# ALiBi attention: both heads' products ahead of both mask records, on the diagonal blocks

## The reference, cut to what matters

```
scores = einsum('bqhd,bkhd->bhqk', q, k) * scale
bias   = slopes[:, None, None] * rel            # rel = key position - query position
scores = where(rel <= 0, scores + bias, -inf)   # causal
probs  = softmax(scores, axis=-1)
attn   = einsum('bhqk,bkhd->bqhd', probs, v)
```

## Time and profile before

| | us |
|---|---|
| median of three runs | 1590.12 (1585.02 to 1590.92) |
| the profiled execution | 1588.67 |
| its span | 1586.8 |
| its mean granted TensorE clock | 0.966 |
| PE busy | 1477.9 (93% of the span) |
| DVE busy | 893.4 (56%) |
| ACT busy | 805.4 (51%) |
| POOL busy | 549.5 (35%) |

### The profile page before, as it was taken

The page is one execution under the profiler, slowest core; times in us unless marked ns, Lnnn a source line. Parts: engine busy times, 40 slices in busy tenths (PEclk is TensorE's granted clock), DMA queues, the critical chain, the costliest instruction groups (busy, mean ns, idle before and its releaser), DMA issues. The chain is left out here.

```text
span 1586.8 us, 23991 instructions
## 1 busy us (share of the span) xinstructions
PE 1477.9 (93%) x8320; PEld 1036.9 (65%) x8320; DVE 893.4 (56%) x1346; ACT 805.4 (51%) x1731; POOL 549.5 (35%) x506
## 2 busy tenths in 40 slices
PE   5499999999999999999968988899999989999996
PEld 4377676667767766776635866555555548888885
DVE  3145454555544555554565745666666616877877
ACT  2266555556655555666423430455555565433343
POOL 0444433344443334444015044223232004444442
PEclk9699999999999999999978997999999999999998
DMA  3135544544454354445530034333333205000000
GB/s 120 49 46 51 50 34 47 42 40 43 48 50 34 46 47 40 39 46 41 84 60 1 1 44 69 48 55 55 55 55 55 88 2 226 1 1 0 1 27 27
DMA packets 46289, 74.06 MB, mean 47 GB/s; under 512 B 18704, under 2 KB 24848, under 8 KB 45328
## 3 DMA queue, kind: packets, MB, share of 16 engines
q1 hardware_dynamic: 41872, 62.70, 28.4%
q0 software_dynamic: 4352, 10.49, 4.4%
HBM read 40.39 MB, written 2.10 MB: 27 GB/s over the span
## 5 line engine op out<-in xcount | busy, mean ns | idle before, releaser
L677 DVE TENSOR_REDUCE nmax<-sc 128x1 f32<-128x128 f32 (+7 forms) x256 | 192.4, 752 | 182.7 <-PE sc L465 182.7
L1515 DVE TENSOR_REDUCE pm<-l_sm 128x2 f32<-128x1024 f32 (+1 forms) x192 | 179.8, 957 | 112.6 <-PE l_sm L1395 61.8
L1475 ACT ACTIVATE l_probs<-l_banks 128x512 f32<-128x512 f32 (+3 forms) x384 | 171.2, 493 | 136.1 <-PE l_banks L1419 97.1
L608 ACT COPY pt<-tb 128x512 f32<-128x512 f32 (+3 forms) x256 | 129.2, 505 | 201.4 <-PE tb L479 199.8
L600 ACT ACTIVATE probs<-sc,nmax 128x128 f32<-128x128 f32 (+7 forms) x256 | 190.6, 745 | 56.2 <-DVE nmax L677 55.9
L479 PE MATMUL tb<-ident,probs 128*128 128x128 f32 x1152 | 174.1, 276 | 2.1 <-ACT pt L608 1.1
L78 PE MATMUL sc<-k_h,q_h 128*128 128x512 f32 (+3 forms) x384 | 144.7, 377 | 22.1 <-POOL q_l L748 14.6
L1416 PE MATMUL l_banks<-qk_bufs 128*128 128x512 f32 (+3 forms) x384 | 141.3, 412 | 5.2 <-ACT l_probs L1475 3.8
L1392 PE MATMUL l_sm<-qk_bufs 128*128 128x512 f32 (+3 forms) x384 | 130.8, 412 | 12.9 <-DVE pm L1515 6.5
L503 PE MATMUL mb<-pt,ckv 128*64 128x512 f32 (+3 forms) x768 | 137.8, 494 | 0.1
L78 PE MATMUL sc<-k_l,q_h 128*128 128x512 f32 (+3 forms) x384 | 133.7, 348 | 0.0
(11 more groups left out here) (263 smaller groups left out, 3145.2 us busy)
## 6 DMA issues: line engine op xcount, KB each, us to landing
gated_late<-in_gated SPq DMA_DIRECT2D x11, 768.0 KB, 14.0
wout<-in_w_out SPq DMA_DIRECT2D x16, 512.0 KB, 7.1
late<-late SPq DMA_DIRECT2D x128, 64.0 KB, 2.0
rb<-rT SPq DMA_DIRECT2D x64, 128.0 KB, 8.8
qk_bufs<-late SPq DMA_DIRECT2D x96, 64.0 KB, 5.0
qk_bufs<-late POOLq DMA_DIRECT2D x96, 64.0 KB, 5.9
nope_t<-in_nope_by_dim SPq DMA_DIRECT2D x16, 192.0 KB, 5.6
late<-in_gated SPq DMA_DIRECT2D x3, 768.0 KB, 9.1
```

What stands on the lines that cost most here:

```text
L608: act.copy(pt[i // 4][:, e, j0:j0 + nb, (i % 4) * P:(i % 4 + 1) * P], tb[TB[g]][:, 0:nb, :]).then_inc(pt_act, 1)
L677: dve.tensor_reduce(nmax[:, n % 4:n % 4 + 1], sc[n % 2][:, 0:(n // 2 + 1) * P], AX.X, ALU.max, negate=True).then_inc(negmax, 1)
L1475: act.activation(probs[(NC * g + c) % RING][:, h, 0:w], banks[:, (E_STEPS * g + n) % SLOTS, 0:w], ACT.Exp).then_inc(exped, 1)
L1515: dve.tensor_reduce(pm[g % 2][:, :, s, i, half], slot(("m", g, n))[:, :, 0:w], AX.X, ALU.max, negate=True).then_inc(freed, 1)
```

## The change

In `m`, the two products of a diagonal unit come first and their two mask records behind them. In `e`, the products of two heads on a diagonal block are issued at the place of the even head (h0 or h2), then both mask records; the place of the odd head (h1 or h3) is empty. Work that the order puts between the two heads therefore follows behind the pair. Each mask record still raises `sE` once, so that ACT takes the same steps in the same order. Since the pair writes two banks, it waits at its first product until one more exponential is done: product n waits for exponential n-2, not n-3.

```diff
@@ -1391,7 +1391,8 @@
                     for par in range(2):
                         last = pe.matmul(dst[:, par, 0:w], queries(b, s)[:, i * P:(i + 1) * P], keys(b, 2 * s + par)[:, c0:c0 + w],
                                          start=True, stop=not diagonal)
-                        if diagonal:
+                    if diagonal:
+                        for par in range(2):
                             last = pe.matmul(dst[:, par, w - P:w], keep.ident_b[:], keep.mask[:], start=False, stop=True)
                     last.then_inc(scores, 1)
 
@@ -1411,12 +1412,19 @@
                         pe.wait_ge(rows_in, ROWS * (g + 1))
                         if g == 0:
                             pe.wait_ge(v_ev, ST)
-                    from_one(pe, exped, E_STEPS * g + n + 1 - SLOTS)
                     diagonal = q0 == j * P
-                    last = pe.matmul(banks[:, at, 0:w], keys(b, h)[:, j * P:(j + 1) * P], queries(b, h // 2)[:, q0:q0 + w],
-                                     start=True, stop=not diagonal)
+                    if diagonal and h % 2:
+                        return
+                    both = (h, h + 1) if diagonal else (h,)
+                    from_one(pe, exped, E_STEPS * g + n + len(both) - SLOTS)
+                    for x in both:
+                        last = pe.matmul(banks[:, (at + x - h) % SLOTS, 0:w], keys(b, x)[:, j * P:(j + 1) * P], queries(b, x // 2)[:, q0:q0 + w],
+                                         start=True, stop=not diagonal)
                     if diagonal:
-                        last = pe.matmul(banks[:, at, 0:P], keep.ident_b[:], keep.mask_t[:], start=False, stop=True)
+                        for x in both:
+                            last = pe.matmul(banks[:, (at + x - h) % SLOTS, 0:P], keep.ident_b[:], keep.mask_t[:], start=False, stop=True)
+                            if x == h:
+                                last.then_inc(sE, 1)
                     last.then_inc(sE, 1)
```

## The result

The changed kernel takes 1605.12 us (median; 1604.42 to 1606.65), the kernel before 1590.23 in the same comparison: 1.011 times, with a 95% interval of 1.0082 to 1.0137. The medians differ by 15 us, and the forecast was 1601. The profiled execution has a span of 1602.6 us, 15.8 more than before.

A forecast was written before the change was run, and what follows sets the result against it. PE was taken to bound the second pass, with short waits. Load cover -13.4, bank waits +23.1 and uncashed saving +2.0 make +11.7 us, forecast 1601; its own range 1595 to 1606, the 8-in-10 range 1594 to 1611.

The forecast's parts named there:

- What bounds the kernel: Attention stage: PE bounds the second pass, with short waits, and nothing behind the stage absorbs the difference.
- The load cover: Diagonal pairs in both passes: weight loads hidden behind neighbouring products save 0.02 to 0.07 us a pair, 13.4 us in all.
- The unknown price: A mask record behind a mask record on PE: taken as 0.06 us, the least possible, with 0.11 the next kind above.
- Units side by side: First-pass units that now follow each other wait for DVE's buffers: 2 us of the saving are not cashed.
- The wait for the banks: Second pass: a chunk's second pair waits for h0's exponential, 0.85 to 0.52 us by width; 23.1 us lost in all.
- The groups: Bank waits left after filling, per group: 2.87 us in groups 1, 3, 5; 2.86 in 0, 2, 4; 2.03 in 6.
- The last group: Group 7, with nothing to fill its bank waits: 3.90 us of them, the group some 3 us longer than 27.5.
- The first group: Group 0 of the second pass, counted like groups 2 and 4: 2.86 us lost to bank waits.
- no cover: Rival, chance 0.03: loads of a product behind a product are not hidden in the pair; +25 us, 1614.
- the dear mask record: Rival, chance 0.15: a mask behind a mask costs 0.11 us, each pair loses 0.05 more; 1610 us.
- no change: Rival, chance 0.15: bank waits run together with existing waits and half of the 23.1 us vanishes; 1589 us.
- faster: Rival, chance 0.05: bank waits cost nothing because the exponentials are done in time; 1577 us.

The follow-up runs named there:

- e1: Kernel before with only the first pass (`m`) paired, the second pass as before: 1580.39 us, 0.996 of before.
- e11: Kernel before with pairs only in the second pass of the last group: 1594.5 us, 1.0046 of before.
- e8: Kernel before with first pass paired and second-pass mask records put behind the two products of a first-pass unit standing next: 1580.76 us, 0.9957 of before.
- e7: Changed kernel with seven unread 512-column products in PE's idle time ahead of the last group's second pass: 1598.56 us, 1.0069 of before.

## Why the prediction was right, and where its sum was short

**What bounds the kernel: right.** PE's order and its short waits. Groups with pairs whose waits are filled got shorter, groups with holes longer, and nothing behind the stage took up the difference (282.8 us against 282.2).

**The load cover: right in kind and nearly in size.** 0.84 us a group less what is lost in DVE waits was summed for the first pass, 0.59 net; measured are 0.51 to 0.78 in groups 1 to 6, 4.05 / 6 = 0.68. The unknown price, mask behind mask, came out at 0.07, near the lower bound. The rule of the Trainium skill ("TensorE: Matmul & The Clock Gate"), by which no load would be covered among matmuls of all rows, stands in its section "The mechanism", not in the one that the prediction names; it would have left e1 unchanged, and e1 gained 0.4%. The same section also says that a load can run ahead into the background weight buffer, and the cover measured here agrees with that.

**Units side by side: about right.** 2 us were summed. Between 950 and 1325 us the first pass's loads waited for DVE 34 times in e1 and 40 times in the changed kernel, where it was 23, and PE's own idle time there grew from 6.5 to 8.2 and 9.2 us.

**The wait for the banks: right, and to a hundredth in the open place.** Between the first and the third product 1.49, 1.29, 1.06 and 0.88 us were worked out, from exponentials and mask starts of before. In c8 to c11 of the last group they are 1.50, 1.27, 1.05 and 0.87. These chunks run at full clock, and from chunk start to chunk start c8, c9 and c10 take 3.28, 2.94 and 2.40 us against 2.76, 2.55 and 2.10: 0.52, 0.39 and 0.30 more, where 0.65 - 0.12, 0.55 - 0.12 and 0.43 - 0.14 stood in the sum. One reading was wrong and carried nothing: the third product of c8 stood 0.74 us behind the first before, not 0.88, which is from the second (1296.22) to the fourth (1297.10).

**The groups.** Odd groups: 2.87 of holes, 1.68 of cover and 0.25 of DVE waits make +1.44; measured +1.33. Groups 2 and 4: 2.86, the same sum, +1.43; measured +1.55. Group 6: +0.60 was summed and +1.61 came. This term was a third of its size. The maxima's transpose, which starts the transfers for which the last group waits, comes 1.41 us later in the group (34.17 against 32.76 us behind its start), so the holes ahead of it were more than I counted, and the time from there to the next group grew by 0.2 as well. About half of the 1.41 lies in c10: the list had the transpose between h2 and h3, now it follows the whole second pair, and from the start of c10 to it there pass 1.52 us instead of 0.79. The rest is spread over c0 to c9 and was not taken apart.

**The last group: the step that is missing.** 3.90 of holes less 0.84 of cover, +3.1, was summed, from holes at full clock, and +8.06 came. In c8 to c11 the sum holds, as shown; in the first chunks the clock is at half. c0, c1 and c2 take 3.53, 4.76 and 5.43 us against 2.12, 2.67 and 2.95. With what c8 to c10 lost at full clock added to the times of before they would have taken 8.95 us; they took 13.72. The prediction had read the clock at 1.00 and did not ask what idle time would do to it; 5 us of the 15.8 are that. What brings the fall about is not shown. Only that pairs in this group cost more than their holes at full clock is, by e11: 7.8 us by the medians.

**The first group.** +1.43 was summed for it, and 0.59 of gain for the units of its own first pass, which lie ahead of it: +0.84 up to the start of group 1. The profiled executions show 0.35 less (1039.39 against 1039.74). This is made of two parts. Group 0 took 44.50 us instead of 41.61, but its first 4.3 us were at half clock, in the kernel before none; from its third chunk on, at full clock in both, it lost 0.98 us, as group 2 did there (1.02). And its first product came 3.2 us earlier; e11, with the code of before up to there, was 3.8 us earlier, so this says nothing of the edit. The group's own term is borne out, the total up to group 1 is not settled.

**The sum.** 11.7 was the sum, and 15.8 came: group 6 gave 1.0 more, the last group 5.0 more, the stretch up to group 1 1.2 less and the stage behind 0.7 less. The last two are within what executions of the same code differ by, so part of the error was made good by chance. 1605.12 lies in the forecast's own 1595 to 1606, but near its edge, with 5 us from a mechanism that the prediction does not have. (1590.12 and 11.7 make 1602, not 1601; this changes nothing.)

**The signs and the rivals.** The second pass was to last near 317 us and lasted 325.6 (994.9 to 1320.5), since the clock, group 6 and group 0's half clock are in it. The last group was to last 3 us longer and lasted 8.1. One sign came out for the wrong rival: products of a pair over 0.3 us apart were to mean no cover, and they are 0.34 apart at 512 columns (c8). The sign was badly chosen. A product behind a wait takes 0.34 us up to its mask before the change as well (1297.10 to 1297.44); in the pair h0's product stands 0.58 ahead of the first mask, so h1's product added 0.24, the covered price. Of the rivals, the dear mask record falls with its 0.07, no change and faster with the rows of the holes, no cover with e1.

## What to carry to other kernels

Covering a weight load by putting products side by side is worth the uncovered part of the load, here 0.06 us a place; a pair that needs two buffers at once out of three loses several times that (0.52 to 0.85 us) as soon as nothing stands behind it to fill the wait. Take the cover from an instruction that needs no further buffer (the other pass here), and pair only where the buffer is free in time. Work out a hole from the start of the consumer's first input to its end plus both hand-overs, at every width, and then ask what the idle time does to the clock of the engine that has the hole.

## What the runs showed of the hardware

Two 128-column bf16 matmuls with the same stationary operand, each with its load, start 0.07 us apart (the two masks take 0.29 us together, one alone 0.22 to 0.23). A fp32r product of 512 columns behind another costs 0.23 us; with a mask record between them they stand 0.35 apart, 0.12 more.

The granted clock of TensorE fell to 1.2 GHz in the last group in nine of thirteen profiled executions. In the changed kernel PE was busy for 3.08 of the 5 us ahead of it (1280 to 1285), with 1.61 us idle in one piece. An idle time of 1.35 or 1.36 us there went without a fall in three kernels (before, e1, e8) and was followed by one in e11. In e7 the longest idle time in the 12 us ahead of the fall was 0.63 us. The clock came back after 3.4, 6.8 or 13.7 us. The cost in the last group was about 5 us for 13.7 us at half clock (an estimate: 8.06 less the 3.1 summed), while ACT's exponentials, for which the group also waits, took as long as before (two of 512 columns 1.09 us at full clock and 1.08 at half).
